# Routing of the last token group cut into pieces, tile tables beside the statistics, and the expert weights split between ACT and POOL

## What is computed

```python
x = layernorm(x + first_block(x))
probs = softmax(x @ Wg)                     # 8 experts
weights, indices = top_k(probs, 2)
for e in range(8):
    h = gelu(x @ W1[e] + b1[e])
    out = out + (h @ W2[e] + b2[e]) * cw[:, e:e + 1]
out = layernorm(x + out)
```

## Time and profile before

| what | value |
|---|---|
| median of 3 runs | 338.85 us (338.72 to 339.04) |
| profiled execution, its own time | 338.63 us |
| its span in the trace | 336.6 us |
| busy: PE, DVE, ACT, POOL | 271.1, 231.3, 210.6, 220.2 us |
| POOL's share of the chain that ended last | 45% |

### The profile page before, as it was taken

One profiled execution on the slowest core, in us unless ns is written; L12 is line 12 of the kernel. 1 busy time (PEld: TensorE's weight loads), 2 busy tenths in 40 slices (PEclk: granted clock), 3 DMA queues, 4 the chain that ended last, 5 costly groups with the idle time before them and its releaser, 6 DMA issues.

```text
span 336.6 us, 5255 instructions
## 1 busy us (share of the span) xinstructions
PE 271.1 (81%) x1287; PEld 210.6 (63%) x1287; DVE 231.3 (69%) x729; ACT 210.6 (63%) x458; POOL 220.2 (65%) x265
## 2 busy tenths in 40 slices
PE   2487999899998749737779699999999999981920
PEld 1333656556645527536679599999999999830400
DVE  3854739968869746916878678888888888600870
ACT  3512245644843745817769599999999999810380
POOL 3999196167778776700277777777777777772580
PEclk9997999999999959969979999999999999997875
DMA  4992010001111153324446465565556555315952
GB/s 89 331 333 74 1 33 1 0 16 49 48 47 39 50 153 115 118 57 179 167 125 242 160 208 198 176 222 195 183 196 219 198 178 177 118 47 177 375 157 62
DMA packets 31366, 46.39 MB, mean 138 GB/s; under 512 B 5097, under 2 KB 23025, under 8 KB 31337
## 3 DMA queue, kind: packets, MB, share of 16 engines
q1 hardware_dynamic: 25620, 35.97, 32.6%
q0 software_dynamic: 4832, 9.97, 8.9%
q10 hardware_dynamic: 884, 0.12, 0.2%
HBM read 16.99 MB, written 13.86 MB: 92 GB/s over the span
## 4 chain that ended last, share of the span: by engine, by line
POOL 45%; issue 18%; PE 13%; DVE 12%; DMA 6%; ACT 3%; SPq 0%; DVEq 0%; ACTq 0%; POOLq 0%
POOL results_d L460 27%; POOL slots_d L454 15%; PE bank L1076 3%; DVE work L694 3%; DVE early L973 1%; DMA late<-slots_d 1%; DMA slots_d<-rows,slot_i 1%; PE bank L1164 1%; PE bank L1053 1%; POOL rstd L443 1%; PE bank L1054 1%; DMA rows<-results_d 1%; DMA logs<-in_L_attn_nu_log_dram 1%; PE bank L1022 1%; PE bank L1055 1%
## 5 line engine op out<-in xcount | busy, mean ns | idle before, releaser
L460 POOL DMA_INDIRECT results_d<-work,dest x87 | 92.1, 1059 | 26.5 <-issue 26.5
L454 POOL DMA_INDIRECT slots_d<-rows,slot_i x64 | 65.6, 1025 | 41.5 <-DVE rows L833 21.9
L591 ACT ACTIVATE h<-bank,buse 128x384 f32<-128x384 f32 x116 | 68.0, 586 | 13.5 <-PE bank L1024 8.2
L924 DVE TENSOR_TENSOR h_l<-h,h_h 128x384 fp32r<-128x384 f32 x116 | 65.2, 562 | 15.7 <-ACT h_h L596 13.1
L1022 PE MATMUL bank<-h_h,wuse 128*128 128x384 f32 x116 | 45.0, 388 | 5.6 <-DVE h_l L924 5.4
L1022 PE MATMUL bank<-xbt_h,wuse 128*128 128x384 f32 x116 | 40.9, 353 | 2.3 <-ACT h L591 2.3
L1023 PE MATMUL bank<-xbt_l,wuse 128*128 128x384 f32 x116 | 39.7, 342 | 0.0
L1024 PE MATMUL bank<-xbt_h,wuse 128*128 128x384 f32 x116 | 39.6, 342 | 0.0
L1024 PE MATMUL bank<-h_h,wuse 128*128 128x384 f32 x116 | 39.6, 341 | 0.0
L1023 PE MATMUL bank<-h_l,wuse 128*128 128x384 f32 x116 | 39.4, 340 | 0.0
L528 ACT ACTIVATE h<-bank 128x512 f32<-128x512 f32 x32 | 18.8, 597 | 28.7 <-PE bank L1024 28.1
(11 more groups left out here) (199 smaller groups left out, 573.1 us busy)
## 6 DMA issues: line engine op xcount, KB each, us to landing
wuse<-fw SPq DMA_DIRECT2D x29, 512.0 KB, 3.4
late<-slots_d SPq DMA_DIRECT2D x29, 195.0 KB, 2.5
fw<-in_L_ffn_W_dram SPq DMA_DIRECT2D x16, 256.0 KB, 6.3
work<-in_L_attn_x3d_dram SPq DMA_DIRECT2D x8, 256.0 KB, 5.4
rows<-results_d SPq DMA_DIRECT2D x4, 512.0 KB, 5.3
work<-results_d SPq DMA_DIRECT2D x4, 512.0 KB, 8.6
out_dram<-fw SPq DMA_DIRECT2D x8, 256.0 KB, 2.3
slots_d<-zeros SPq DMA_DIRECT2D x9, 195.0 KB, 6.5
```

Of the source, the lines that this page charges most:

```text
L454: pool.indirect_dma_start(out=slots_d, out_offset=bass.IndirectOffsetOnAxis(ap=slot_i[:, k, i:i + 1], axis=0), in_=rows[:, k, i, :], in_of ...
L460: pool.indirect_dma_start(out=results_d, out_offset=bass.IndirectOffsetOnAxis(ap=dest[:, SQ * g + q:SQ * g + q + 1], axis=0), in_=yo[:, g ...
L591: act.activation(h32[:, b % 2, 0:SLOTS], H_PS[b % 2][:, 0:SLOTS], ACT.Gelu, bias=buse[:, k, b:b + 1]).then_inc(sm["gelu_b"], 1)
L924: dve.tensor_tensor(ht_l[b], h32[:, b % 2, 0:SLOTS], ht_h[b].bitcast(F32), ALU.subtract).then_inc(sm["hbl_ready"], 1)
```

## The change

The groups stay four groups of two chunks, now written as bounds (0, 2, 4, 6, 8), from which slices and waits are derived. What moves:

- The cast of each expert weight goes from POOL to ACT (`weights_high`), four per chunk in chunks 0 to 3, two ahead of the cast of `y` and two behind it. POOL keeps the subtract (`weights_low`).
- POOL's `norm` keeps the power alone; the negation and the multiply become one DVE instruction (`offsets`), which waits for the power. DVE's separate negated mean is gone.
- A finished group's weights come at the head of the next chunk, and `route_tiles` directly behind the statistics, ahead of the logits' copy.
- `first_tile` becomes `first_weights` without the low part of tile 0 and its slots' data; these stand behind the residual of chunk 7. PE transposes chunk 7's residual first, then tile 0, then multiplies the logits; tile 1 is transposed inside step 0.
- Group 3's routing: choice ahead of step 0, ranks and slots ahead of step 1, exponential on ACT ahead of step 2, weights ahead of step 3, the table ahead of step 5.

```diff
-GC = 2
+BOUNDS = (0, 2, 4, 6, 8)
...
 # POOL
-            def weights(e, a):
...
-                pool.tensor_copy(fw_part(e, a, 0), raw).then_inc(sm["fw_hi"], 1)
+            def weights_low(n):
+                e, a = divmod(n, 2)
+                pool.wait_ge(sm["fw_hi"], n + 1)
+                pool.tensor_tensor(fw_part(e, a, 1), fw_part(e, a, 1).bitcast(F32), fw_part(e, a, 0).bitcast(F32), ALU.subtract).then_inc(sm["fw_lo"], 1)
             def norm(c):
-                pool.wait_ge(sm["nm_ready"], c + 1)
-                wait(pool, sm["row0_ready"], c)
+                pool.wait_ge(sm["ve_ready"], c + 1)
                 pool.tensor_tensor(rstd[:, QT * c:QT * (c + 1)], var_e[:], mhalves[:], ALU.pow).then_inc(sm["rstd_ready"], 1)
-                pool.wait_ge(sm["rstd_ready"], c + 1)
-                pool.tensor_tensor(nmr[:], nmean[:], rstd[:, QT * c:QT * (c + 1)], ALU.mult).then_inc(sm["nmr_ready"], 1)
...
-            for e in range(E):
-                for a in range(2):
-                    weights(e, a)
-                if e in (4, 6, 7):
-                    norm((4, 6, 7).index(e))
+            for n in range(NFW):
+                if n in (4, 8, 12):
+                    norm(n // 4 - 1)
+                weights_low(n)
...
 # ACT
+            def weights_high(n):
+                e, a = divmod(n, 2)
+                act.wait_ge(fw_loaded[e], 32)
+                act.copy(fw_part(e, a, 0), fw_part(e, a, 1).bitcast(F32)).then_inc(sm["fw_hi"], 1)
...
-            walk(act, MT, step, {1: lambda: rows_of(NCH - 1), 3: second_exp,
+            walk(act, MT, step, {1: lambda: rows_of(NCH - 1), 2: second_exp,
...
 # DVE
+            def offsets(c):
+                dve.wait_ge(sm["rstd_ready"], c + 1)
+                wait(dve, sm["row0_ready"], c)
+                dve.scalar_tensor_tensor(out=nmr[:], in0=mv[:, :, 0], scalar=-1.0, in1=rstd[:, QT * c:QT * (c + 1)],
+                                         op0=ALU.mult, op1=ALU.mult).then_inc(sm["nmr_ready"], 1)
...
+                if ended is not None:
+                    route_weights(ended)
                 if c >= 1:
-                    if g is None and c >= 3:
-                        route_weights(routed_in(c - 1))
                     stats(c - 1)
                     aggregate(c - 1)
+                    if ended:
+                        route_tiles(ended - 1)
                     logits(c - 1)
...
-                dve.wait_ge(sm["route_ready"], 1)
+                dve.wait_ge(sm["route_ready"], 2)
...
-                x_low(0, 0)
-                meta(0, 0)
...
+            x_low(0, 0)
+            meta(0, 0)
             stats(NCH - 1)
...
-            walk(dve, MT, step, {1: last_choice, 2: last_slots, 4: last_weights})
+            walk(dve, MT, step, {0: last_choice, 1: last_slots, 3: lambda: route_weights(NG - 1), 5: last_tiles})
...
 # PE
+                if g == 0:
+                    xt(1, 1)
...
+            r_transposed(NCH - 1)
+            xt(0, 0)
+            logits(NCH - 1)
             pe.wait_ge(sm["w1use_ready"], 1)
             pe.wait_ge(sm["xb_lo"], 1)
             hidden(0, 0, 0)
             hidden(0, 0, 1)
-            r_transposed(NCH - 1)
-            logits(NCH - 1)
-            xt(1, 1)
...
-                pe.wait_ge(sm["row0_ready"], NCH)
+                pe.wait_ge(sm["lg_sb"], NCH)
                 ranks(NG - 1)
-            walk(pe, MT, step, {2: last_ranks})
+            walk(pe, MT, step, {1: last_ranks})
```

More of the change, by code:

```diff
@@ L67, in build @@
     NT = T // P
-    NG = NCH // GC
-    GT = GC * QT
-    pairs = [2 * GT * P * (g + 1) for g in range(NG)]
+    NG = len(BOUNDS) - 1
+    GT = QT * max(b - a for a, b in zip(BOUNDS, BOUNDS[1:]))
+    pairs = [2 * QT * P * b for b in BOUNDS[1:]]
     MT = (pairs[-1] + E * (SLOTS - 1)) // SLOTS
@@ L111, in build @@
         jio = sb("jio", [P, 2, MMAX])
-        restart = sb("restart", [P, E * GT])
+        sizes = sorted({QT * (b - a) for a, b in zip(BOUNDS, BOUNDS[1:])})
+        restart = {n: sb(f"restart{n}", [P, E * n]) for n in sizes}
         zeros = sb("zeros", [P, SQ * ROW])
@@ L259, in build @@
         GROUP = kept // 3
-        assert kept % 3 == 0 and ends[PHASES - 2] <= kept
+        assert kept % 3 == 0
         dispatched = [sem(f"dispatched{i}") for i in range(NG)]
@@ L269, in routed_in, with tokens_of @@
         def routed_in(c):
-            return (c - 2) // GC if c >= 2 and c % GC == 0 else None
+            return BOUNDS.index(c) - 1 if c in BOUNDS[1:] else None
+        def tokens_of(g):
+            return QT * BOUNDS[g], QT * (BOUNDS[g + 1] - BOUNDS[g])
         def fw_part(e, a, part):
@@ L350, in _ @@
                 sp.wait_ge(sm["route_ready"], n + 1)
-                sp.wait_ge(dispatched[n + 1], 16 * 2 * GT)
+                sp.wait_ge(dispatched[n + 1], 16 * 2 * tokens_of(n + 1)[1])
                 for g in range(begins[n], ends[n]):
                     load(g, g % 2)
-                    if g == 1:
-                        sp.wait_ge(sm["fw_lo"], NFW)
-                        second_weights(0)
                     if g == 2:
                         sp.wait_ge(sm["pre_a"], HB * NCH)
-                    if g >= 2 and g not in begins:
+                    if g not in begins:
                         second_weights(g - 1)
@@ L461, in send_back @@
                                             in_=yo[:, g % YO, q, :], in_offset=None).then_inc(returned[min(g // GROUP, 3)], 16)
-            for e in range(E):
-                for a in range(2):
-                    weights(e, a)
-                if e in (4, 6, 7):
-                    norm((4, 6, 7).index(e))
-            for g in range(NG - 1):
-                dispatch(g, 0)
-                if GC * g + 3 < NCH:
-                    norm(GC * g + 3)
-                dispatch(g, 1)
-                if GC * g + 4 < NCH:
-                    norm(GC * g + 4)
-            for half in range(GC):
-                dispatch(NG - 1, half)
+            for n in range(NFW):
+                if n in (4, 8, 12):
+                    norm(n // 4 - 1)
+                weights_low(n)
+            for g in range(NG - 1):
+                dispatch(g, 0, 4)
+                norm(2 * g + 3)
+                dispatch(g, 4, 8)
+                if 2 * g + 4 < NCH:
+                    norm(2 * g + 4)
+            dispatch(NG - 1, 0, 8)
             for g in range(MT):
@@ L724, in chunk @@
             def chunk(c):
-                g = routed_in(c)
+                g, ended = routed_in(c), routed_in(c - 1)
                 if c + 1 < NCH:
@@ L942, in last_choice @@
                 route_choice(NG - 1, 0)
+                offsets(NCH - 1)
                 route_choice(NG - 1, 1)
```

128 lines of the change are left out of this document (66 added, 62 removed).

## The result

The changed kernel took 329.6 us (median of 4 runs, 328.72 to 331.71) beside 338.79 us for the kernel before. The ratio is 0.9745, with an interval of 0.971 to 0.9781: faster, by some 9 us where 14 were forecast.

A forecast was written before the change was run, and what follows sets the result against it. The prediction took POOL's chain of dispatches and sends as the bound: group 3's dispatch 15.0 us earlier (5.2 of it from group 2's last dispatch), sends 0.9 slower, so 14.1 less, 324.5 us, range 319 to 328.

The forecast's parts named there:

- The weights' part: Group 3's routing: POOL starts its dispatch 7.1 us after tile 3, where it was 16.9; bounds 5.7 to 9.5.
- its 6.1: Time in us from tile 3 to step 2's end on DVE, taken between 8.5 before and a steady step's 4.7.
- the set-up's own gain: Casts moved from POOL to ACT shorten chunks 0 and 1 by 5.4 us; bounds nothing to some 6.
- the norm: Multiply moved from POOL to DVE: 1.2 us saved between dispatches, 2.1 at the fifth norm with its wait for statistics.
- The cast of y for chunk 4 moves from 70.39 to 65.0: On ACT, the set-up's 5.4 us was to carry through to chunk 4.
- dispatches from 69.2: POOL's first dispatch, behind four last subtracts at 1.27 us each, 1.9 us earlier than 71.13.
- the casts on ACT: Sixteen casts of 0.62 us, four per chunk, costed at nothing on the chunk chain; 9.9 us without cover.
- nothing was new: DVE's offset waits for POOL's power in chunks 2, 4 and 6, where the exponents waited before; no cost.
- The sends: POOL's sends of results: about ten more at the slow pace beside tile work, adding 0.9 us.
- The final stage: From the last send to the end, 32.5 us, left as it is.
- The set-up gives nothing: Rival: chunk 0 and 1's long pairs are DVE's own start; dispatch at 74.6, 329.9 us, chance 0.13.
- Slower: Rival: each subtract in chunks 0 to 3 may stop DVE 1.41 us; 347.0 us if all sixteen do, chance 0.05.

The follow-up runs named there:

- late_group: The change with the last group's choice, ranks, exponential and weights back at their old steps 1 to 4; 338.46 us, ratio 0.9998.
- dve_low_next: The change with subtracts on DVE, casts earlier, chunk 1's offset between group 0's choices, POOL's powers re-placed, last group's exponential in step 1; 317.26 us.
- multiply_back: The change with the offset's multiply back on POOL and the negative mean from DVE, casts still on ACT; 328.62 us.
- offset_first: The change with chunk 1's offset multiplied on DVE between group 0's two choices instead of behind the whole routing; 326.00 us.
- half_low: The change with POOL leaving out the last eight of sixteen subtracts, a diagnostic and no candidate; 317.78 us.
- quarter_low: The change with POOL leaving out the last four of sixteen subtracts, a diagnostic and no candidate; 325.41 us.
- old_setup: The change with casts, subtracts and the offset's multiply back on POOL, the last group's routing still in pieces; 325.18 us.
- early_casts: The change with ACT casting eight halves each in chunks 0 and 1, so POOL's subtracts run earlier; 322.60 us.

## Why the prediction was right in part and wrong in part

**Right: the bound and the last group.** POOL's chain set the time: from group 3's first dispatch to the last send it waited for nothing but its own issue. The weights' part, tile 3 to group 3's dispatch, was put at 7.1 us and measured 7.10. Choice and ranks came before tile 3, as said, and late_group shows that without the pieces nothing is gained. That the figure agrees to the digit is luck: its 6.1 was taken between two bounds, and the exponential did not fit into ACT's pause as the forecast had it. DVE stood 2.88 us behind it, and dve_low_next, which moves it ahead, needs 6.09. Tile 9 followed tile 3 by 35.5 us (37 forecast), and ACT's last rows tile 9 by 104.0 (104.1), so PE didn't decide.

**Right: the set-up's own gain.** 5.4 us forecast, 4.9 found at y's cast for chunks 1 and 2, the pairs at 1.29. (The subtract at 24.57 of the earlier trace rows, which the prediction lays beside chunk 1's pair, ended as that pair began; beside the pair ran a cast at 26.61 and a subtract at 27.29, so the reading holds.) Also the norm: from the first dispatch to group 2's last 68.50 us instead of 71.19, 2.7 less where 3.3 were forecast; POOL's last two powers still waited 0.16 and 0.50 us for statistics.

**The step that failed: "The cast of y for chunk 4 moves from 70.39 to 65.0" and with it "dispatches from 69.2".** Measured: 69.77 and 73.63. This one step is 4.4 of the 5.0 us by which group 2's last dispatch missed (142.13 for 137.1); the norm is the other 0.6. It has two halves.

The first half is what lies between chunks 2 and 4. The prediction priced the casts on ACT at nothing, and multiply_back shows that this was right: 65.10. It also said of chunk 2 that nothing was new, since the exponents had waited for the same power before. It looked at what stands behind the offset on DVE. It should have looked at what stands ahead of it, group 0's whole routing, and at who waits for it, ACT's rows and, behind them, the exponential, its tables, the gelus of chunk 3 and PE. The prediction put this wait at nothing. The routing is short when nothing disturbs it, and the subtracts in chunk 2 stretched it, as POOL's weights had in the kernel before, where no offset stood behind it. It takes both: offset_first, by moving the offset alone, brings the cast to 66.11 and 3.6 us back; half_low, without the stretch, has it at 64.37; quarter_low, with stretch and offset left in, keeps it at 69.53.

The second half is a term left out. With y's cast where the forecast had it (multiply_back), the dispatch still began at 71.22, not 69.2. Chunk 2's power stands on POOL ahead of the last four subtracts and waits for the statistics until 63.89, so these begin at 65.12 and not at 63.7 (0.2 of that is the multiply of this run), and the four took 5.90 us instead of 4 x 1.27. In the change itself this half lies hidden under the first: the power was done at 65.62, and the subtracts waited 2.11 us more for ACT's late casts. old_setup's 325.18 lies beside the forecast's 324.5, but by another way, without the set-up's gain that the forecast counted on, so it is no support for it.

**Smaller terms.** Group 3's first dispatch missed by 5.4 us (155.87 for 150.5) and the last send by 4.0 (294.04 for 290.0). The sends were to cost 0.9 more; from group 3's first dispatch to the last send it took 138.17 us, 0.4 less. 81 sends lay beside tile work, 80 before: the tile stage moved with them. The final stage took 32.06 us, 0.4 less than before. A time here can be told from no change by some 0.35%, the half interval of the result, and not by 0.2%.

**The rivals.** "The set-up gives nothing" named 329.9 us and a dispatch at 74.6, close to the 329.60 and 73.63 measured. That is luck: its condition, long pairs that are DVE's own start, did not hold (1.29 us), and the gain was there at chunks 1 to 3 and lost behind them. "Slower" had the right mechanism and the wrong price: it counted held instructions against a whole subtract each, when what mattered was which ones. Four of them, 3.7 us, were enough because of what queued behind. That the change lost part of its gain, and did not come out slower, goes with the pieces (late_group, 338.46).

Left open: how much of chunk 3's delay is the queue behind the offset and how much PE's lower clock after the wait; the runs move both together. Also open is what the reordering that old_setup and late_group both keep is worth by itself, and where the median of old_setup lies ahead of its own profile.

## What to carry to other kernels

Before work is moved to an idle engine, ask what the old place hid: POOL's casts were slow but early, and the quicker split left its last pieces in front of the instruction that sets the end. An instruction of 0.15 us that moves to another in-order queue takes on the delay of all that stands ahead of it, so its price is read from its consumers' waits. When two chains are late, each repair has to be tried alone and with the other: here the two repairs by order nearly add up (3.6 and 7.0 us alone, 11.1 together), while the two halves of the old set-up gave some 1 us each alone, not clear of noise, and 4.4 together.

## What was not expected of the hardware

Of DVE's instructions beside POOL's subtracts, those with two inputs were stretched, 0.22 to 1.26 us and 0.27 to 1.32, while a reduction with one input between them, at 52.15, kept its 0.22. The Trainium skill, "SBUF — State Buffer", section "Who interferes with whom", states that a DVE instruction with two SBUF inputs contends with a POOL instruction that reads SBUF, and that a reduction on this chip does not; the trace agrees, with those numbers. The one-input addition at 50.10 in early_casts (L715) took 1.13 us beside subtracts and 0.17 in the change; the same section of the Trainium skill counts such additions with a scalar among those that can enter a two-port mode, and so contend, when their operands meet certain conditions. The longer time fits that; no run here shows which mode the instruction was in.

The four subtracts that met the routing took 5.01 us, four times the 1.26 of one that nothing stretched: POOL lost nothing and DVE 3.7 us. In multiply_back four of them took 5.90, so POOL can pay as well.
